# Four layers on one adjacency matrix: the load in another order, normalisation shared with GpSimd, W3's sign moved, widening a head earlier

## What is computed

```python
h = max(layernorm(x), 0); gt = adj.T
deg = sum(gt, axis=1)                                   # layer 0: sums over columns of adj
x = x + (deg**-.5)[:,None] * gt * (deg**-.5)[None,:] @ (h @ W0) + b0
h = max(layernorm(x), 0)                                # layer 1
head = (adj > 0); head = head / max(sqrt(sum(head*head, -1)), EPS)
inc = adj + head;  x = x + (inc @ h) / sum(inc, -1)
h = max(layernorm(x), 0)                                # layer 2: 4 heads of 256
ht = h @ W2; e = leaky_relu(src[:,None] + dst[None,:]) + adj
x = x + mean over heads of softmax(e) @ ht
h = max(layernorm(x), 0)                                # layer 3
x = x + relu(adj @ (max(sign(h), 0) @ sign(W3).T))
```

## Time and profile before

| | us |
|---|---|
| median of 3 runs | 708.93 (708.64 to 709.93) |
| profiled execution, its own time | 708.1 |
| its span in the trace | 706.3 |

### The profile page before, as it was taken

How to read it: one execution, slowest core, us unless ns; L and a number is a source line. 1 busy time by engine, 2 the same in 40 slices (tenths; PEclk the granted TensorE clock), 3 DMA queues, 4 the chain that set the end, 5 groups by cost and what they waited for, 6 DMA issues and landing times.

```text
span 706.3 us, 15923 instructions
## 1 busy us (share of the span) xinstructions
PE 685.5 (97%) x6416; PEld 585.8 (83%) x6416; DVE 619.0 (88%) x1134; ACT 458.4 (65%) x784; POOL 112.2 (16%) x146
## 2 busy tenths in 40 slices
PE   3899999999999999999999999999999999999998
PEld 3786888888888864488888888888888888888887
DVE  5998999958989968899999999999999899994672
ACT  3895158639898327975559776686865878654650
POOL 3005623321133110002100012100211000000000
PEclk9999999999999999999999999999999999999999
DMA  9996999993799967589988799998999893474391
GB/s 337 375 363 262 425 425 270 315 247 122 209 283 237 227 171 206 164 179 207 238 199 233 140 233 240 240 248 173 194 245 222 232 207 82 76 190 140 131 309 38
DMA packets 167000, 159.53 MB, mean 226 GB/s; under 512 B 115536, under 2 KB 128528, under 8 KB 160912
## 3 DMA queue, kind: packets, MB, share of 16 engines
q1 hardware_dynamic: 145568, 100.32, 53.1%
q0 software_dynamic: 19056, 41.42, 26.1%
q10 hardware_dynamic: 2304, 16.78, 5.7%
HBM read 69.86 MB, written 52.46 MB: 173 GB/s over the span
## 4 chain that ended last, share of the span: by engine, by line
PE 83%; DVE 8%; ACT 4%; issue 4%; DMA 1%; POOL 0%; SPq 0%; ACTq 0%; POOLq 0%; DVEq 0%
PE ps L843 15%; PE ps L845 15%; PE ps L844 15%; PE ps L780 6%; PE ps L890 4%; PE ps L889 4%; PE ps L678 3%; PE ps L677 3%; PE ps L676 3%; DVE arena L1260 2%; DVE arena L1343 2%; PE ps L725 1%; DMA arena<-adj_t 1%; PE ps L727 1%; PE ps L726 1%
## 5 line engine op out<-in xcount | busy, mean ns | idle before, releaser
L843 PE MATMUL ps<-arena 128*128 128x257 f16 x1024 | 279.9, 273 | 1.3 <-DVE arena L1483 1.3
L845 PE MATMUL ps<-arena 128*128 128x257 f16 x1024 | 279.4, 273 | 0.0
L844 PE MATMUL ps<-arena 128*128 128x257 f16 x1024 | 279.2, 273 | 0.0
L1176 ACT ACTIVATE arena<-arena 128x512 f16<-128x512 f32 x252 | 158.3, 628 | 97.9 <-PE ps L845 79.6
L1476 DVE SCALAR_TENSOR_TENSOR arena<-arena,w_j 128x512 f32<-128x512 f32 x256 | 190.1, 743 | 0.0
L1483 DVE TENSOR_TENSOR arena<-arena 128x512 f16<-128x512 f32 x256 | 175.7, 687 | 9.1 <-ACT arena L1176 8.8
L843 PEld LDWEIGHTS ps<-arena 128*128 128x128 f16 x1024 | 99.9, 98 | 14.3 <-ACT arena L1176 1.5
L844 PEld LDWEIGHTS ps<-arena 128*128 128x128 f16 x1024 | 100.3, 98 | 12.6
L845 PEld LDWEIGHTS ps<-arena 128*128 128x128 f16 x1024 | 99.8, 97 | 12.9
L725 PE MATMUL ps<-arena 128*128 128x257 f16 x256 | 70.3, 275 | 0.0
L727 PE MATMUL ps<-arena 128*128 128x257 f16 x256 | 69.8, 272 | 0.0
(11 more groups left out here) (149 smaller groups left out, 1061.2 us busy)
## 6 DMA issues: line engine op xcount, KB each, us to landing
adj_t<-arena POOLq DMA_DIRECT2D x32, 1024.0 KB, 7.7
arena<-in_adj_dram SPq DMA_DIRECT2D x30, 1024.0 KB, 6.0
adj_parts<-arena ACTq DMA_DIRECT2D x16, 1024.0 KB, 21.6
arena<-adj_t SPq DMA_DIRECT2D x64, 256.0 KB, 4.9
arena<-adj_t SPq DMA_DIRECT2D x10, 1024.0 KB, 6.5
x<-arena POOLq DMA_DIRECT2D x15, 512.0 KB, 6.2
arena<-u_rows SPq DMA_DIRECT2D x4, 1024.0 KB, 14.5
x<-in_x_dram SPq DMA_DIRECT2D x4, 512.0 KB, 5.6
```

The source lines that it names most:

```text
L843: mm(ps[:, bank, 0:DE], hi, ht_hi[:, head, j, 0:DE], start=s, stop=False)
L844: mm(ps[:, bank, 0:DE], hi, ht_lo[:, head, j, 0:DE], start=False, stop=False)
L845: ins = mm(ps[:, bank, 0:DE], lo, ht_hi[:, head, j, 0:DE], start=False, stop=e)
L1176: nc.scalar.activation(p_hi[:, j % 4, :], prob[:, j % 4, :], copy).then_inc(p_hi_done, 1)
```

## The change

- SP loads quarters 0 and 1 of x, then the first half of row 0 of `adj`, quarter 2 and W0, the second half, quarter 3, and then the other rows. W3 is loaded behind piece 10 and no longer behind layer 0, and the wait for `y_ps` before it is gone.
- The normalised blocks lie in `hw[t]`, each its own place, which `hw_copy(t)` overwrites later. Blocks 1 to 3 of every quarter are normalised by GpSimd, behind the quarter's power; block 0 by VectorE behind pieces 0, 2, 4 and 7 (`NORM_AFTER`). VectorE no longer waits for TensorE's transposes there.
- `unread` is 1 per piece for pieces 1 to 13, 6 for pieces 14 to 16, and 8 behind the last; it was 2 for pieces 1 to 16 and 6.
- W3's sign: the first comparison stands before VectorE's wait for the degrees, the second right behind the copy of the degrees; TensorE transposes at j = 6 of layer 0 into bank 5, ScalarE copies behind `g_hi`. All of it is gone from layer 1.
- `WIDEN_AFTER`: block 12 behind group 6 (was 7), 13 behind 7 (was 8), 14 and 15 behind 8 (15 was behind 9).

```diff
-        WIDEN_AFTER = {0: (6,), 1: (7,), 3: (8,), 4: (9, 10), 5: (11,), 7: (12,), 8: (13, 14), 9: (15,)}
+        WIDEN_AFTER = {0: (6,), 1: (7,), 3: (8,), 4: (9, 10), 5: (11,), 6: (12,), 7: (13,), 8: (14, 15)}
@@ SP
-            reload_rows(8)
-            sp.wait_ge(y_ps, NB)
-            sp.dma_start(w3_f, w3_d.rearrange("(c p) d -> p c d", p=P)).then_inc(w3_in, 16)
-            for t in range(9, 12):
+            for t in range(8, 12):
@@ GpSimd, behind each quarter's power
+                pool.wait_ge(rstd_done, p + 1)
+                for t in range(XP * p + 1, XP * p + XP):
+                    nc.gpsimd.tensor_scalar(hw[:, t, :], x[:, t, :], mean_var[:, t, 0:1], rstd[:, t:t + 1],
+                                            ALU.subtract, ALU.mult).then_inc(pool_normed, 1)
@@ TensorE
-                    unread(2)
+                    unread(1 if n < row_slot(NB - 1) + 2 else 6)
             ins.then_inc(deg_done, 1)
-            unread(6)
+            unread(8)
...
             for j in range(NB):
+                if j == 6:
+                    turn_w3()
                 pe.wait_ge(g_lo_done, j + 1)
@@ ScalarE
+                if t == 4:
+                    act.wait_ge(w3_signed, 1)
                 nc.scalar.activation(g_hi[:, t, :], hw[:, t, :], copy,
                                      scale=dinv_in[:, t:t + 1]).then_inc(g_hi_done, 1)
+            act.wait_ge(w3_t_ps, 1)
+            nc.scalar.activation(bw_t[:, :, :].rearrange("p c d -> p (c d)"), ps16(5)[:, 0:DC * D], copy
+                                 ).then_inc(w3_t_done, 1)
@@ VectorE
-                if t % XP == 0:
-                    dve.wait_ge(rstd_done, t // XP + 1)
-                if t >= 2:
-                    dve.wait_ge(h0_t_ps, t - 1)
-                v.tensor_scalar(h0_n[:, t % 2, :], x[:, t, :], mean_var[:, t, 0:1], rstd[:, t:t + 1],
+                dve.wait_ge(rstd_done, t // XP + 1)
+                v.tensor_scalar(hw[:, t, :], x[:, t, :], mean_var[:, t, 0:1], rstd[:, t:t + 1],
                                 ALU.subtract, ALU.mult).then_inc(normed, 1)
...
+            below_w3()
             dve.wait_ge(deg_done, 1)
             v.tensor_scalar(deg[:, :], ps[:, 4, 0:NB], 2.0 ** -16, None, ALU.mult).then_inc(deg_copied, 1)
+            sign_w3()
```

More of the change, by code:

```diff
@@ L127, in gnn_stack @@
         w0_f = view(G0, [DC, D], F32)
[L128 to L130 removed]
+        w3_f = view(G0 + 2 * KB, [DC, D], F32)
+        w3_s = view(161 * KB, [DC, D], F16)
         b0_bc = view(160 * KB, [D], F32)
@@ L356, in load_x @@
                 sp.dma_start(x[:, XP * p:XP * p + XP, :], x_rows[:, XP * p:XP * p + XP, :]).then_inc(x_in[p], 16)
-            for p in range(4):
-                load_x(p)
-            sp.dma_start(w0_f, w0_d.rearrange("(c p) d -> p c d", p=P)).then_inc(w0_in, 16)
+            load_x(0)
+            load_x(1)
             for n, (j, lo, hi) in enumerate(PIECES):
@@ L765, in _ @@
                         h2_transposes(t - 2)
-                    if g == 1 and t == NB - 1:
-                        turn_w3()
                     if g == 3 and t == 15:
@@ L1262, in adj_low @@
                                        nat[:, lo:hi, 0, j, :], ALU.mult, ALU.subtract).then_inc(nat_lo_done, 1)
-            for p in range(4):
+            for p in range(3):
                 x_stats(p)
```

39 lines of the change are left out of this document (21 added, 18 removed).

## The result

| | before | after |
|---|---|---|
| median, us | 708.43 (706.45 to 709.93, 8 runs) | 712.67 (711.10 to 717.16, 8 runs) |
| profiled execution, us (span) | 708.1 (706.3) | 717.16 (715.4) |

The change makes the kernel slower: ratio 1.0072, interval 1.0052 to 1.0091, against a forecast of 705.8 us.

The account below looks back on a forecast made before the run. Most of the chain of waits was TensorE's, also the fullest engine in the load. Terms -1.5 + 0.5 - 0.8 - 1.3 = -3.1 took 708.1 to 705.0; with 0.8 for the median, 705.8 us, range 703.9 to 709.2.

Parts of the forecast that it names:

- Term 1: Load: moving normalisations to GpSimd shortens the cycle from 8.59 to 7.95 us, -1.5 us (ends -2.3 and +2.5).
- the fullest: Load after the change: VectorE's cycle of three rows, at 7.7 us, was taken as the fullest engine's.
- No wait in these rows is for a DMA: Load before the change: the prediction's reading of the three engines' timelines over the 8.59 us cycle.
- six `unread`: Load's tail: TensorE, with six `unread` of 0.215 us behind pieces 14 to 16, is late next; degrees end at 58.1.
- The third rival: Load's tail: the clock falls behind eight `unread`, layer 0 starts at 1.2 GHz, +1.7 us, 707.5; chance 0.11.
- Term 2: Step into layer 0: W3's second comparison holds GpSimd's power, +0.5 us (0 to +0.6).
- Term 3: End of layer 1: without W3's sign and transposes TensorE starts 0.82 us earlier, -0.8 us (-0.6 to -2.5).
- the second rival: End of layer 1: with the gap closed TensorE's clock may stay at 2.4 GHz, 704.2 us; chance 0.12.
- Term 4: Third refill of `e_in`: sooner widening leaves the refill the DMA alone, -1.3 us (0 to -1.3).
- the fourth rival: Layer 2: sooner widening only moves the wait, to the seventh add, costing 0 to 0.5; 707.6 if refill stays late; chance 0.11.
- The first rival: Load: GpSimd's norms hold VectorE 0.46 us each or longer, late powers too; 709.7, or 712.6 at 0.7; chance 0.16.

Follow-up runs that it names:

- powers-first run: Changed kernel with GpSimd's four powers ahead of all twelve normalisations; 710.54 us, ratio 1.0047.
- one-of-four run: Kernel before with normalised blocks in hw's rows, GpSimd normalising one block of four and VectorE the other three; 705.83 us, ratio 0.9970.
- second profile of the same kernel: Changed kernel run again without an edit; 714.40 us, ratio 1.0083; the profiled execution took 716.36 us.
- all on VectorE: Changed kernel with all sixteen normalisations on VectorE, still into hw's rows; 707.56 us, ratio 0.9983; variants of it were also run.
- rows, W3, widening: Kernel before plus all sixteen normalisations by VectorE into hw's rows, W3's sign in the load and the sooner widening; 705.73 us, ratio 0.9964.
- the best kernel: Kernel before plus all sixteen normalisations by VectorE into hw's rows and W3's sign in the load, old widening; 704.54 us, ratio 0.9945.

## Why the prediction was wrong

The sign was wrong, and one term did it.

**Term 1, -1.5: failed; the profile has +9.1.** The failing step is the price of GpSimd's normalisation. It was bounded as time that it *holds VectorE* (0.14 to 0.46 us), and its own time was set at about 0.4. The rows that it rested on were good: the 1.08 us at 94.22 showed GpSimd, not VectorE, being held. But GpSimd's own cycle was never added up, since GpSimd was idle before. A normalisation takes 1.21 us alone, three times the 0.4, and even so three and a power would be 4.7 us and fit in the 7.95. It is the standing that doesn't fit. One instruction per adj_low, as the prediction itself put it for the rival, is three in a cycle of three rows, which leaves no room for the power. In fact two of three took far longer, 3.48 and 4.69 us: 9.36 + 1.0 = 10.4 us, the 10.46 of the cycle. The powers-first run shows that this pace costs 3.0 us even with the powers out of its way; the one-of-four run shows that it costs nothing once it fits. VectorE itself was held less than the 0.22 per normalisation: in three rows one start of adj_low came 0.20 us late. By medians GpSimd's part is 5.1 to 6.8 us, and the load's order 1.2 to 1.8, where the prediction had row 1 land as before: it reaches ScalarE 1.1 to 1.2 us later. The rest of the profile's 9.1 us is clock and the longer tail. Over the whole kernel the parts by medians, -2.8 for the two-buffer wait, +5.6 for GpSimd, +1.2 to 1.8 for the order and -1 for W3, add up to some 3 to 4 us; 4.2 (712.67 - 708.43) and 6.5 (714.40 - 707.93) were measured, so about 3 us of the second are in no term.

A second step of the same term was wrong and would have stood even with a free GpSimd: VectorE as "the fullest" after the change. It is the two-buffer wait alone that paid, with 2.8 us, more than the 1.5 of the whole term. Behind it the transfers (share 1.00), TensorE and ScalarE are full by their shares, and twelve normalisations fewer gain nothing. "No wait in these rows is for a DMA" (the 1.38 us at 14.87 lie ahead of the cycle) was read as room; a DMA share of 0.95 to 0.97 in the windows from 20 to 50 us said how little there was.

Late next: six `unread`, as forecast. VectorE's last adj_low ends at 65.86 us and the copy follows 3.2 us later, of which 2.3 was forecast; the rest is a granted clock of 0.50 from 62 to 65, where six of them took 2.72 us in place of 1.46. In the second profile of the same kernel the clock stays at 1.00 there, and the copy follows by 2.3. The third rival, a fall of the clock behind the eight `unread` that puts layer 0 at 1.2 GHz, came in none of the seven profiles that have them.

**Term 2, +0.5: absent at the first product here, nearly right where its conditions held.** In the changed kernel W3's second comparison began 0.2 us after the power:

```profile
69.08 0.17 DVE L1285 TENSOR_SCALAR deg<-ps 128x16 f32<-128x16 f32 x1 [2.88 <-PE ps L631]
69.53 0.69 DVE L1248 SCALAR_TENSOR_TENSOR arena<-arena 128x512 f16<-128x512 f32 x1 [0.28 <-issue]
...
69.33 4.40 POOL L529 TENSOR_TENSOR dinv_in<-deg,neg_half 128x1 f32<-128x1 f32 x4 [18.64 <-DVE deg L1285]
```

Copy to first product took 2.11 us (2.13 before). In the kernels with all on VectorE the comparison followed the copy at once, and the step was 2.51 us (58.36 to 60.87 in "rows, W3, widening"): +0.38. By the last product of layer 0 the changed kernel is 0.2 us later behind the copy than before (13.3 and 13.1 us), the others 0.3 to 0.4. Why the comparison waited 0.27 to 0.29 us ("issue") in all four profiles with GpSimd's twelve and W3 in the load, and in none of the five with all on VectorE, stays open.

**Term 3, -0.8: right,** with the second rival on top. The step from the start of layer 1's last product to that of the first 512-column one is 3.16 to 3.34 us in the eight profiles with the sign in layer 1 and 2.48 to 2.75 in the nine with it in the load; the four transposes' 0.22 us inside layer 1 are gone as well. The clock's 1.3 to 1.7 us come on top in four of the eight. By the medians it is about -1.

**Term 4, -1.3: right in its place, wrong in its sum.** The refill's wait went, and the fourth rival's wait came, by its own chain: the add behind block 12, ScalarE standing 1.4 to 5.0 us in eight of the ten profiles with the sooner widening. The prediction gave TensorE three steps of 1.3 us in hand for it and took 0 to 0.5; it lost nothing in the first profile after and up to 2.3 in others.

The first rival had the right suspect and late powers among its terms. Its time near the result (712.6) is luck: the larger part of its sum slowed VectorE, and no adj_low took longer than 2.52 us in any of the profiles (2.29 alone).

## What to carry to other kernels

Before work goes to an idle engine, add up that engine's cycle with its instructions at the length they have beside the others, not alone, and look for what stands behind them in its queue. Then ask whether the engine that is relieved was the limit: take the work away altogether (transpose x itself) and time that, for it is the most that moving it can bring. Of a wait on two buffers, the buffers are the cheap cure: here it was worth 2.8 of the 3.8 us that the best kernel gained.

## What the runs showed of the hardware

- A GpSimd tensor_scalar on 128x256 f32 takes 1.21 us with two scalars per partition from SBUF and 1.07 with constants when VectorE leaves it alone. Beside adj_low (two arena operands, 2.29 us) it takes up to 4.7 and 2.63 us, once 7.56 (with scalars). The Trainium skill, "SBUF — State Buffer", section "Who interferes with whom", has a VectorE instruction with two SBUF inputs contend with a GpSimd instruction that reads SBUF, the later one blocked for the whole of the other. On GpSimd's side the trace agrees: the 3.48 us of the first of three are its 1.21 and one adj_low. The 4.69 and the 7.56 are longer than one blocking makes them. On VectorE's side it doesn't show: of each three adj_low one started 2.41 us behind the one before instead of 2.20, where a whole normalisation would be 1.2 us.
- TensorE's granted clock varies from execution to execution. The load is the same in the kernel before and in the one with the sooner widening alone: from 20 to 30 us the clock is 1.00 in the one profile and 0.83 in the other, and the copies are at 59.95 and 62.64. A single profile of this load is good to about 3 us, so the copies in the table order the runs less well than the medians.
- The layer-1 stretch of the first profile after (TensorE busy 19.04 and 18.05 of 20 us) came again in the run with the new order alone, and in no other: there GpSimd waits 8.8 to 10.1 us in layer 2's additions (4.3 before, 3.8 to 4.8 in the others), with layer 1's powers queued behind. What starts it stays open.
